# A 64-head Toeplitz convolution on TensorE: one row transfer per head for the second pair, and small kernel matmuls moved inside every fourth pair

## What is computed

```python
K = 2.0 * jnp.einsum('hn,hnl->hl', Cs, jnp.exp(P)).real      # 64 filters of 1024 taps
u_m = u * mask[:, None, :]
y = jnp.fft.irfft(rfft(u_m, n=2L) * rfft(K, n=2L))[..., :L]  # causal convolution per head
y = y + u_m * D[:, None]
return y * mask[:, None, :]
...
x = x + attn(conv(x))          # Q, K, V projections, softmax attention, output projection
x = x + ffn(mix(x))            # per-condition channel mix, dense layer plus gated low-rank experts
```

## Time and profile before

| what | us |
| --- | --- |
| median of 3 runs | 875.67 |
| the profiled execution | 874.4 |
| its span (first to last instruction) | 872.6 |
| TensorE busy in it | 853.4 |
| VectorE, ScalarE, GpSimd busy | 464.7, 221.4, 449.0 |
| convolution, first L652 to last | 20.9 to 162.8 |

### The profile page before, as it was taken

One profiled execution on the slowest core, in us unless ns is written; L12 is line 12 of the kernel. 1 busy time (PEld: TensorE's weight loads), 2 busy tenths in 40 slices (PEclk: granted clock), 3 DMA queues, 4 the chain that ended last, 5 costly groups with the idle time before them and its releaser, 6 DMA issues.

```text
span 872.6 us, 24726 instructions
## 1 busy us (share of the span) xinstructions
PE 853.4 (98%) x10922; PEld 740.5 (85%) x10922; DVE 464.7 (53%) x898; ACT 221.4 (25%) x377; POOL 449.0 (51%) x346
## 2 busy tenths in 40 slices
PE   3999999999999999999999999999999999999998
PEld 2899999988888888887777777777779999999998
DVE  6556541122522222238887777888845755545444
ACT  4546543100000000023133223333334322211220
POOL 3344445502377555649968888887746422102220
PEclk9999999999999999999999999999999999999999
DMA  3777878514254322254634454546436211222211
GB/s 92 179 198 196 207 201 206 186 49 147 101 178 125 87 73 73 49 180 135 159 106 150 146 182 157 171 166 186 135 133 225 97 64 57 77 98 98 97 50 49
DMA packets 96907, 114.90 MB, mean 132 GB/s; under 512 B 44064, under 2 KB 66336, under 8 KB 96800
## 3 DMA queue, kind: packets, MB, share of 16 engines
q1 hardware_dynamic: 93808, 112.29, 42.9%
q10 hardware_dynamic: 2480, 0.51, 0.3%
q0 software_dynamic: 512, 0.53, 0.2%
HBM read 80.16 MB, written 33.13 MB: 130 GB/s over the span
## 4 chain that ended last, share of the span: by engine, by line
PE 96%; DMA 1%; DVE 1%; SPq 1%; issue 0%; ACT 0%
PE ps L988 25%; PE ps L1277 21%; PE ps L1599 15%; PE ps L652 10%; PE ps L1627 5%; PE ps L952 5%; PE ps L663 4%; PE ps L1233 3%; PE ps L1213 3%; PE ps L1509 2%; PE ps L1644 1%; PE ps L1643 1%; SPq L608 1%; DMA kpad<-ksb 1%; DMA toep<-kpad 0%; PE ps L1611 0%
## 5 line engine op out<-in xcount | busy, mean ns | idle before, releaser
L1599 PE MATMUL ps<-wb_hi,xf 128*128 128x424 f32 x440 | 127.0, 356 | 0.0
L988 PE MATMUL ps<-y_hi,w_hi 128*128 128x512 f32 x320 | 125.1, 391 | 0.0
L988 PE MATMUL ps<-y_hi,w_lo 128*128 128x512 f32 x320 | 124.5, 389 | 0.0
L988 PE MATMUL ps<-y_lo,w_hi 128*128 128x512 f32 x320 | 124.5, 389 | 0.0
L1575 POOL TENSOR_TENSOR xf<-xs,xf 128x512 fp32r<-128x512 f32 x32 | 42.1, 1345 | 124.8 <-DVE xs L1563 124.8
L1277 PE MATMUL ps<-y_hi 128*128 128x512 f32 x256 | 102.9, 402 | 0.0
L1277 PE MATMUL ps<-y_hi,y_lo 128*128 128x512 f32 x256 | 100.2, 391 | 0.0
L1277 PE MATMUL ps<-y_lo,y_hi 128*128 128x512 f32 x256 | 100.1, 391 | 0.0
L652 PE MATMUL ps<-xc,toep 64*128 64x192 f32 (+4 forms) x1088 | 96.8, 330 | 1.2 <-DMA toep<-kpad 1.2
L652 PEld LDWEIGHTS ps<-xc,toep 64*128 64x128 f32 x1088 | 90.2, 187 | 4.7 <-issue 1.6
L1599 PEld LDWEIGHTS ps<-wb_hi,xf 128*128 128x128 f32 x440 | 82.7, 188 | 2.3
(11 more groups left out here) (190 smaller groups left out, 1618.5 us busy)
## 6 DMA issues: line engine op xcount, KB each, us to landing
toep<-kpad SPq DMA_DIRECT2D x124, 136.0 KB, 3.7
xc<-in_dram SPq DMA_DIRECT2D x32, 256.0 KB, 4.2
q_rows<-rf SPq DMA_DIRECT2D x32, 256.0 KB, 2.6
q<-q_rows SPq DMA_DIRECT2D x16, 512.0 KB
xr<-in_dram SPq DMA_DIRECT2D x16, 512.0 KB, 4.5
x_scratch<-xr SPq DMA_DIRECT2D x16, 512.0 KB, 2.7
x<-x_scratch SPq DMA_DIRECT2D x16, 512.0 KB, 4.1
out_dram<-x SPq DMA_DIRECT2D x15, 512.0 KB, 2.8
```

The source lines that it names most:

```text
L988: mm = pe.matmul(kq_bank(n), w[a][:, j, :], yt[b][:, j, g * 512:(g + 1) * 512], start=(j == 0 and a + b == 0), stop=(j == NJ - 1 and a == 1))
L1599: mm = pe.matmul(dst[:, PLAIN:], xf(i, idx, a)[:, t, :], wb(c, idx, t), start=(start and t == 0 and a + c == 0), stop=(t == 3 and a == 1), ...
```

## The change

The rows of pair 1 are loaded as one transfer of 1088 columns for each head, where before two of 544 columns did it. The count that TensorE waits for on the buffer's semaphore (`rows_landed`) follows. And `kernels_pe` for the groups 2 to 7 stands inside the pairs 3, 7, ..., 23, between their narrow and their wide matmuls, where before it stood behind them.

```diff
         ROW_HALVES = [(0, (L + HALF) // 2), ((L + HALF) // 2, L + HALF)]
 
+        def row_pieces(n):
+
+            return [(0, L + HALF)] if n == 1 else ROW_HALVES
+
         def rows_landed(n):
 
-            earlier = n // TR
-            whole = 16 * 2 * len(ROW_HALVES)
-            return whole * (earlier + 1) if n % TR else 16 * 2 + whole * earlier
+            return 16 * 2 * sum(len(row_pieces(m)) if m > 0 else 1 for m in range(n % TR, n + 1, TR))
...
             for r in range(2):
-                for lo, hi in ROW_HALVES:
+                for lo, hi in row_pieces(n):
                     load_rows(sp, n, r, lo, hi, ld_toep[n % TR])
...
                 if n == 1:
                     kernels_pe(pe, 1)
+                if n % GP == 3 and n // GP + 2 < NHG:
+                    kernels_pe(pe, n // GP + 2)
                 for d, c in WIDE[1:]:
                     mm = wide(pe, n, c, d, start=False, stop=((d, c) == WIDE[-1]))
...
             for n in range(S // 2):
                 convolve(pe, n)
-                if n % GP == 3 and n // GP + 2 < NHG:
-                    kernels_pe(pe, n // GP + 2)
```

## The result

The changed kernel takes 878.98 us (median of 11 runs, 877.5 to 880.32) where the kernel before takes 875.42 (11 runs): a ratio of 1.0032, 95% interval 1.0024 to 1.0041. The medians lie 3.6 us apart (their quotient is 1.0041, the upper end of that interval); by the ratio it is 2.8 us. Forecast were 873.3 us and 2.4 us faster, in a range of 871.5 to 875.0. The kernel before spreads over 874.05 to 877.87 in its 11 runs; its profiled execution, at 874.4, lies 1.0 under their median. The profiled execution has a span of 877.2 us, 4.6 more than before.

The account below looks back on a forecast made before the run. TensorE's sequence was taken as the bound. Cheaper filter sets (1.98 us) and an earlier start (0.4) made 2.4 us off the profiled 874.4; taken from the median 875.67 this gave 873.3 us, range 871.5 to 875.0.

Parts of the forecast that it names:

- What bounds the kernel: TensorE's sequence, 96% of the chain; two convolution waits, 0.7 and 1.2 us, and everything behind pair 2 back to back.
- The sets' price: Six filter sets between narrow and wide matmuls cost 0.26 us each, not 0.59: 0.33 saved a set, 1.98 us in all.
- the prediction's own sign: Wrong on the sets if a wide run between an odd and an even pair is longer than 6.0 us.
- The step that failed: Pair 3's wide part and mask end 0.26 us later, but VectorE waits for TensorE there, so nothing is late.
- The rows of pair 1: At the start SP issues two transfers, not four, 1.28 us less; rows and stores land about 0.4 us earlier.
- b = 0.4: At the start, b is how much earlier pair 2 comes, with rows and stores landing about 0.4 us earlier.
- two rules of the Trainium skill: At the start: fixed 2.0 us plus bytes gives the upper bound; transfers interleaving on the same 16 engines gives nothing.
- The lower bound of 0: Least gain at the start from pair 1's rows, if the window 21 to 22 us is slow for another reason.
- The margin of 0.12 us: In pair 3 the set's tables are ready 0.12 us before the moved set would want to start.
- The first set's pause: Pause behind the first set's fifth matmul, 0.37 us; bounds 0 and 0.37 gained, 0 taken.
- The rivals: Start issue-bound or pause gone (0.40); transfers hidden anyway (0.12); sets not cheaper (0.05); set waits for tables (0.04).
- The slower one: In every fourth pair the moved set waits for its tables; 878.3 us, chance 0.04.

Follow-up runs that it names:

- The fourth experiment: Kernel before, sets in their old place, but the end of pairs 3, 7, ..., 23 signalled from inside the set behind them; 876.66 us, ratio 1.0013.
- the third: Kernel before with the filter sets moved and a third input buffer, so input loads stand behind a pair's rows on SP; 872.67 us, ratio 0.9962.
- 2: Kernel before with the moved filter sets alone, pair 1's rows in halves; 876.83 us, ratio 1.0010.
- 14: Changed kernel with forty repeated waits on a landed constant ahead of TensorE's first matmul; 877.98 us, ratio 1.0027.
- 5: Kernel before with the third input buffer alone, rows in halves and sets in their old place; 874.92 us, ratio 0.9988.
- 1: Changed kernel with the sets back in their old place, so the row change alone; 876.88 us, ratio 1.0014.
- 6: Changed kernel with the third input buffer, so input is loaded ahead; 874.07 us, ratio 0.9983.
- 7: Rows-only version with three useless matmuls on TensorE between pair 1 and pair 2; 876.51 us, ratio 1.0015.
- 8: Rows-only version with the four stores of the second half's filters moved on SP in front of pair 1's rows; 875.01 us, ratio 0.9993.
- 9: Rows-only version with twelve small warm-up matmuls in front of pair 0 replaced by three long ones; 878.11 us, ratio 1.0026.
- 10: Kernel before with twelve small warm-up matmuls replaced by three long ones; 878.36 us, ratio 1.0034.
- the sixteenth: Changed kernel with the third input buffer and the filter stores in front of pair 1's rows; 873.35 us, ratio 0.9973.
- 15: Kernel before, rows in halves and sets in their old place, with the four filter stores in front of pair 1's rows; 875.71 us, ratio 1.0001.

## Why the prediction was wrong, step by step

- **What bounds the kernel.** Right that TensorE's sequence does, and that only two waits stood in it. Wrong in what followed: "Everything behind pair 2 is back to back" was taken as if nothing there could come too late, and there was little to spare. No row of mine said how long before its use a pair's rows had landed.
- **The sets' price.** Right. 0.19 us between narrow end and wide start was forecast and measured, a set in the new place saved 0.34 us of a group's time (forecast 0.33), and the gain of all six is 2.25 us (forecast 1.98) between two versions that differ in nothing else. One of the six wide runs was longer than 6.0 us (6.44), by the prediction's own sign a mark against this term; the measured price stands even so.
- **The step that failed** is the one on what is late from the moved sets: "Pair 3's wide part, and so its mask, ends 0.26 us later than it would; VectorE waits for TensorE in this stage, so nothing is late from it." I followed that end to VectorE alone. SP waits for the same signal: it frees the row buffer and the input buffer of pair 6. Behind the pair the set was 0.59 us of work that ran while SP issued and the DMA engines moved; inside the pair it runs before they may start. The window went from 8.4 + 0.59 = 9.0 us to 8.4 (for pair 6 from 9.4, since the first set has its pause), and the loads take 8.5 or, with a long issue among them, 9.0 to 10.7. The fourth experiment made waits with the signal alone, the third removed them with earlier input loads. Over all eighteen traces a wait in front of pair 6 stands in the four that have the shorter window and two input buffers (the changed kernel, 2, 4, 14) and in none of the others. The waits for rows in front of the even pairs from 4 on add up to 1.98 to 3.57 us in these four, to 0 to 1.57 in the eight with the sets and the signal in their old place, and to nothing in the six with a third input buffer. Shown is the window as a cause and the cure; that it is the whole loss is not: the signal alone costs 1.3 us, the moved sets 3.4 before their gain. The long issues in these chains are a part of the waits' size. TensorE's faster pace, with the same bytes to be moved in less time, may be another, argued only.
- **The rows of pair 1.** SP's saving was forecast at 1.28 us and came to 1.29; pair 1's rows did land earlier (TensorE started on them at 25.20, not 26.08, 0.27 of it the tables'). The forecast b = 0.4 for the stores failed: in this trace the second store landed 0.25 us later, 0.5 counted from the tables. Other traces narrow this down to no gain: with the rows in halves (before, 2 to 5) it landed at 25.78 to 27.02, with one transfer per head (the changed kernel, 1, 6, 7) at 26.43 to 26.82, though issued 1.3 us earlier. The windows of DMA share said how much work there was, not which transfer it would favour: the stores queue behind the rows. Of the two rules of the Trainium skill, "DMA: Bandwidth & Descriptors", that were weighed there, the fixed time plus bytes of "Anatomy of one DMA" would have brought the gain; the trace of the changed kernel disagrees, with 3.8 to 5.5 us for 4 KB. "Issuing engines are not separate DMA queues", by which issue time counts little, is nearer, but gives no loss either. The lower bound of 0 was the wrong bound, since a loss had no place in it. The rows-only version is 1.5 us slower, and experiments 8 and 6 find a loss of that size from two other sides (1.9 and 1.4). Against it stands the pair 9 and 10, which finds none. Each difference is near what an idle edit can do, so that the row change loses something is likely and its size is not shown. How it would lose is partly in view: TensorE idles longer in front of pair 2, and in some executions the granted clock halves for 3.4 us behind that. The prediction had no clock in its sum.
- **The tables.** The margin of 0.12 us in pair 3 was right in place and size: the set began to wait in the third version (0.22) and in the sixteenth (0.66).
- **The first set's pause.** Gone from its place in the changed kernel, but pauses called "issue" of 0.40 us behind the third set and 0.15 us in the fourth came in its stead, so that little of the 0.37 was gained.
- **The rivals.** None had it. The slower one looked for late tables; the rule that a moved signal has more than one reader would have named the right queue.
- **Open.** Why the last share of the stores lands no earlier with long rows, though issued earlier: behind a 16 KB instruction packet on one engine, or behind the rows themselves. Six runs meant to move the packet didn't clear it. Open too is what the long issues are due to.

## What to carry to other kernels

A short piece of work that stands behind a "done" signal is cover for whatever that signal releases. Before it is moved in front, list every queue that waits for the signal, and for each transfer behind it compare the time from signal to landing with the work left until its use; a wait list that shows no wait says nothing about this margin. Ask of the margin also whether it stands one issue that takes a microsecond longer. And a transfer that is issued earlier need not land earlier when something large is ahead of it in the queue: here the place of four 4 KB stores before or behind 544 KB of rows was worth more than 1.3 us of issue time.

## What the runs showed of the hardware that I had not expected

- Four stores of 4 KB each issued just behind 544 KB of row loads took 3.8 to 5.5 us to land, in front of them 2.4 to 3.6.
- An idle time of 2.29 us was followed by a granted clock of 0.50 for 3.4 us in one execution, times of 2.13 and 2.22 us (experiments 6 and 15) likewise, while one of 2.56 us was not. In rows only six of twelve executions have a mean granted clock under 0.999, in the kernel before beside it none of 29.
- An SP issue of usually 0.6 us takes 0.9 to 2.1 us now and then; 304 of 307 such in the first 165 us of the traces overlap with a 16 KB instruction packet on a DMA engine.
- Edits that change only which and how many trivial instructions TensorE has at the start moved the median by 1.2 to 3 us in five of six tries, in three of them with a 1.2 to 1.3 us stall some hundreds of microseconds later.
